# Carrying a product along in the feed-forward cycles instead of computing it again, for half of the tokens

## What is computed

```python
def _twist(x):                      # x in four parts of 64
    o_r, o_i, p_r, p_i = jnp.split(x, 4, axis=-1)
    return jnp.concatenate([p_r, -p_i, -o_r, o_i], axis=-1)

gf = _global_net(x.mean(axis=1, keepdims=True), ...)
out = x
for _ in range(3):                  # NUM_CYCLES
    h = _gelu(out @ w1 + b1)        # 256 -> 256, the "first product"
    h = _gelu(h @ w2 + b2)          # 256 -> 128
    h = _gelu(h @ w3 + b3)          # 128 -> 64
    tf = jax.nn.sigmoid(h @ w4 + b4)            # 64 -> 1
    coupling = 0.1 + adaptive_range * (0.7 * gf + 0.3 * tf - 0.5) * 2.0
    out = out + coupling * _twist(out)
```

## Time and profile before

| | |
|---|---|
| Median of 3 runs | 707.27 us (706.72 to 709.48) |
| The profiled execution | 706.14 us, of which the trace's span is 704.3 us |
| PE busy | 688.3 us (98%) |
| DVE busy | 384.4 us (55%) |
| ACT busy | 287.6 us (41%) |
| Granted PE clock, mean | 0.999 of full speed |

### The profile page before, as it was taken

How to read it: one execution, slowest core, us unless ns; L and a number is a source line. 1 busy time by engine, 2 the same in 40 slices (tenths; PEclk the granted TensorE clock), 3 DMA queues, 4 the chain that set the end, 5 groups by cost and what they waited for, 6 DMA issues and landing times.

```text
span 704.3 us, 11180 instructions
## 1 busy us (share of the span) xinstructions
PE 688.3 (98%) x3616; PEld 475.1 (67%) x3617; DVE 384.4 (55%) x951; ACT 287.6 (41%) x599; POOL 132.9 (19%) x111
## 2 busy tenths in 40 slices
PE   8999999999999999999999999999999999999996
PEld 7777777776754444688999746656556777777765
DVE  4688877788724454788777657212333333333331
ACT  3555434543544655766777541110323222222220
POOL 3100000000000000600000104661123334333333
PEclk9999999999999999999999999999999999999999
DMA  9781000000052000004800201423582666666643
GB/s 292 194 250 34 1 0 0 0 0 0 1 167 73 0 5 5 1 1 167 312 0 1 89 2 49 140 86 113 171 222 30 166 153 175 168 164 164 165 101 35
DMA packets 54934, 65.15 MB, mean 92 GB/s; under 512 B 11583, under 2 KB 37905, under 8 KB 54895
## 3 DMA queue, kind: packets, MB, share of 16 engines
q1 hardware_dynamic: 47806, 55.31, 24.6%
q0 software_dynamic: 7088, 9.35, 7.7%
HBM read 48.48 MB, written 16.00 MB: 92 GB/s over the span
## 4 chain that ended last, share of the span: by engine, by line
PE 92%; DVE 3%; ACT 1%; issue 1%; DMA 1%; POOLq 0%; SPq 0%; DVEq 0%; ACTq 0%; POOL 0%
PE ps L567 82%; PE ps L570 10%; DVE stats L1701 1%; DMA early<-in_wk 1%; DVE x_rows L1965 0%; POOLq L133 0%; ACT work L1285 0%; DVE work L1992 0%; DMA work<-expert_rows 0%; DVE x_rows L2001 0%; DVE work L1834 0%; DVE maxes L1832 0%; ACT early L1448 0%; ACT middle L1319 0%; DVE rden L1990 0%
## 5 line engine op out<-in xcount | busy, mean ns | idle before, releaser
L567 PE MATMUL ps<-middle,work 128*128 128x256 f32 (+4 forms) x656 | 177.4, 420 | 1.2 <-ACT work L1285 0.8
L1285 ACT ACTIVATE work<-ps 128x512 f32<-128x512 f32 (+3 forms) x209 | 83.1, 437 | 200.3 <-PE ps L570 183.6
L567 PEld LDWEIGHTS ps<-middle,work 128*128 128x128 f32 (+1 forms) x656 | 115.7, 183 | 48.3 <-issue 29.2
L567 PE MATMUL ps<-late,work 32*128 32x154 f32 (+5 forms) x880 | 141.9, 345 | 0.6 <-ACT work L1285 0.6
L533 POOL DMA_INDIRECT out_rows<-masks x47 | 70.4, 1498 | 152.3 <-DMA out_rows<-masks 56.7
L567 PEld LDWEIGHTS ps<-late,work 128*128 128x128 f32 (+2 forms) x880 | 92.1, 178 | 6.4 <-issue 3.4
L567 PE MATMUL ps<-work,late 128*128 128x256 f32 (+1 forms) x416 | 83.0, 352 | 0.6 <-ACT work L1285 0.5
L570 PE MATMUL ps<-consts_sb,work 128*128 128x128 f32 (+1 forms) x564 | 80.1, 275 | 1.8 <-DVE work L1992 1.2
L499 POOL TENSOR_TENSOR rstd<-var_eps,minus_half 128x8 f32<-128x8 f32 (+1 forms) x10 | 13.9, 1392 | 358.1 <-DVE var_eps L1716 358.1
L570 PEld LDWEIGHTS ps<-consts_sb,work 128*128 128x128 f32 (+1 forms) x564 | 65.1, 140 | 22.0 <-issue 11.6
L567 PE MATMUL ps<-early,late 128*128 128x512 f32 (+2 forms) x192 | 77.6, 608 | 0.3 <-ACT early L1435 0.3
(11 more groups left out here) (226 smaller groups left out, 720.4 us busy)
## 6 DMA issues: line engine op xcount, KB each, us to landing
late<-in_w SPq DMA_DIRECT2D x40, 512.0 KB
early<-in_w SPq DMA_DIRECT2D x16, 512.0 KB, 9.7
expert_rows<-work SPq DMA_DIRECT2D x36, 130.0 KB, 2.9
work<-expert_rows SPq DMA_DIRECT2D x36, 130.0 KB
middle<-in_w SPq DMA_DIRECT2D x8, 512.0 KB, 7.9
out_rows<-x_rows SPq DMA_DIRECT2D x4, 512.0 KB, 3.2
x_rows<-in_x SPq DMA_DIRECT2D x2, 768.0 KB, 10.6
late<-in_ws SPq DMA_DIRECT2D x3, 512.0 KB, 4.0
```

The source lines that it names most:

```text
L567: return nc.tensor.matmul(o, l, r, start=start, stop=stop, **kw)
L1285: return nc.scalar.activation(o, i, ACT.Copy)
```

## The change

For the second pair of groups the first product is computed from scratch only in the first cycle. There `net1` also computes a second product `z` from the same state with twisted weights `wz` (built once on DVE), which is `_twist(out) @ w1`. ACT copies both products out of PSUM (`keep_y`, `keep_z`). In the later cycles DVE forms the next first product from the kept ones: `turn_y(n)`: y + c z, and between the cycles `turn_z(n)`: z - c y. `act1` of steps 6, 7, 10 and 11 reads the result (`yn`) from SBUF. The state of the second pair is still updated, but nobody on PE waits for it before the end, so its updates move to the back of DVE's list. The first pair keeps computing its products with `net1`.

So PE loses `net1` of steps 6, 7, 10 and 11 (eight calls) and gains four calls for `z` of steps 2 and 3. ACT gains eight copies. DVE gains four small operations for `wz`, four `turn_y` and two `turn_z`, each of the latter four operations of 128x512. `su1` moves to other banks and other places. The orders on all three engines are written out anew, and the two `keep_warm` matmuls stand behind `net3(5)` and `net4(5)`.

```diff
+FIRST = [("y", 0), ("y", 1), ("y", 2), ("y", 3), ("z", 2), ("z", 3), ("y", 4), ("y", 5), ("y", 8), ("y", 9)]
+UPDATES = [0, 1, 4, 5, 2, 3, 6, 8, 9, 7, 10, 11]
...
+        ys = cut(early, 4096, [2, 2, G4]); zs = cut(early, 6144, [2, 2, G4])
+        yn = cut(work, 4608, [2, 2, G4]); turn_u = [cut(work, 3584 + 512 * o, [G4]) for o in range(2)]
+        wz = cut(masks, 1600, [KD, 256])
...
-            def net1(n, o):
+            def net1(n, o, kind="y"):
                 g = ffn_group(n)
-                pe.wait_ge(q["f_upd"], n + 1)
+                if kind == "z":
+                    pe.wait_ge(q["f_ev"], n - 1)
+                elif n < NG:
+                    pe.wait_ge(q["f_upd"], n + 1)
+                else:
+                    pe.wait_ge(q["f_upd"], updated(n - NG))
+                    pe.wait_ge(q["f_ev"], 3 + n % 2)
...
             def net2(n):
                 pe.wait_ge(q["f_a1"], 2 * n + 2)
+                after(pe, q["f_a2"], n - 1)
...
             net2(2)
+            net1(2, 0, "z")
+            net1(2, 1, "z")
             pe.wait_ge(q["f_gact"], 3)
             net2(3)
-
-            for p in range(2, 6):
-                net1(2 * p, 0)
-                net3(p - 1)
-                net1(2 * p, 1)
-                net4(p - 1)
-                net1(2 * p + 1, 0)
-                net1(2 * p + 1, 1)
-                net2(2 * p)
-                net2(2 * p + 1)
-                if p < 4:
-                    su1(p - 2)
-
-            to_rows(0, 0, 0)
-            net3(5)
-            to_rows(0, 1, 6)
-            to_rows(1, 0, 4)
-            to_rows(1, 1, 5)
-            net4(5)
+            net1(3, 0, "z")
+            net1(3, 1, "z")
+            net1(4, 0)
+            net3(1)
+            net1(4, 1)
+            net4(1)
+            net1(5, 0)
+            net1(5, 1)
+            net2(4)
+            net2(5)
+            su1(0)
+            net3(2)
+            su1(1)
+            net4(2)
+            net2(6)
+            net2(7)
+            net3(3)
+            net1(8, 0)
+            net4(3)
+            net1(8, 1)
+            net1(9, 0)
+            net1(9, 1)
+            net2(8)
+            net2(9)
+            net2(10)
+            net3(4)
+            net2(11)
+            net4(4)
...
-            keep_warm(2, 1)
+            net3(5)
+            keep_warm(1, 1)
+            net4(5)
+            keep_warm(1, 1)
+            to_rows(0, 0, 0)
+            to_rows(1, 0, 4)
+            to_rows(0, 1, 6)
+            to_rows(1, 1, 5)
...
             def act1(n, o):
-                act.wait_ge(q["f_l1"], 2 * n + o + 1)
-                nc.scalar.activation(h1[n % 2][:, o, :], ps[:, 4 * (n % 2) + o, :], ACT.Gelu,
+
+                after(act, q["f_l2"], n - 1)
+                if ("y", n) in FIRST:
+                    act.wait_ge(q["f_l1"], first_product("y", n, o))
+                    src = ps[:, 4 * (n % 2) + o, :]
+                else:
+                    act.wait_ge(q["f_y"], turned_y(n, o))
+                    src = yn[:, n % 2, o, :]
+                nc.scalar.activation(h1[n % 2][:, o, :], src, ACT.Gelu,
...
+            def keep_y(n, o):
+
+                last = copy(ys[:, n % 2, o, :], ps[:, 4 * (n % 2) + o, :])
+                if o == 1:
+                    last.then_inc(q["f_ev"], 1)
+
+            def keep_z(n):
+
+                for o in range(2):
+                    act.wait_ge(q["f_l1"], first_product("z", n, o))
+                    last = copy(zs[:, n % 2, o, :], ps[:, 4 * (n % 2) + o, :])
+                last.then_inc(q["f_ev"], 1)
...
             act2(2)
+            keep_z(2)
             act2(3)
-            for p in range(2, 6):
...
+            keep_z(3)
+            act1(4, 0)
...
+            act2(5)
+            act1(6, 1)
+            act3(2)
+            act1(7, 0)
+            act1(7, 1)
+            act4(4)
+            act4(5)
+            act2(6)
+            act2(7)
+            act3(3)
+            act1(8, 0)
+            act4(6)
+            act4(7)
+            act1(8, 1)
+            act1(9, 0)
+            act1(9, 1)
+            act1(10, 0)
+            act2(8)
+            act1(10, 1)
+            act2(9)
+            act1(11, 0)
+            act3(4)
+            act1(11, 1)
+            act2(10)
+            act2(11)
+            act4(8)
+            act4(9)
             act3(5)
             act4(10)
             act4(11)
...
+            def turn_y(n):
+
+                k, c = n % 2, tt[n - NG]
+                dve.wait_ge(q["f_a4"], n - NG + 1)
+                dve.wait_ge(q["f_ev"], 3 + k)
+                seq.mark(v.tensor_tensor(turn_u[0], c, zs[:, k, 0, :], ALU.mult))
+                seq(v.tensor_tensor(turn_u[1], c, zs[:, k, 1, :], ALU.mult))
+                for o in range(2):
+                    v.tensor_tensor(yn[:, k, o, :], (ys if n < 2 * NG else yn)[:, k, o, :], turn_u[o],
+                                    ALU.add).then_inc(q["f_y"], 1)
+                dve.wait_ge(q["f_y"], turned_y(n, 1))
+
+            def turn_z(n):
+
+                k, c = n % 2, tt[n]
+                seq.mark(v.tensor_tensor(turn_u[0], c, ys[:, k, 0, :], ALU.mult))
+                seq(v.tensor_tensor(turn_u[1], c, ys[:, k, 1, :], ALU.mult))
+                for o in range(2):
+                    seq.mark(v.tensor_tensor(zs[:, k, o, :], zs[:, k, o, :], turn_u[o], ALU.subtract))
+                seq.sync()
...
-            for n in range(10):
-                update(n)
...
+            update(0)
+            update(1)
+            turn_y(6)
+            turn_y(7)
+            seq(v.tensor_reduce(odd, con[:, C_BD:C_BD + 8].rearrange("p (a j) -> p j a", j=2), AX.X, ALU.add))
+            su1_build(0)
+            turn_z(2)
+            su1_build(1)
+            update(4)
+            update(5)
+            turn_z(3)
+            turn_y(10)
+            turn_y(11)
+            update(2)
+            update(3)
+            update(6)
+            update(8)
+            update(9)
+            update(7)
             ffn_out(0, 0, 0, 1)
             ffn_out(1, 0, 4, 2)
             variances(5)
```

More of the change, by code:

```diff
@@ L201, in build @@
         h3 = [cut(early, 11264 + 512 * p, [G4]) for p in range(2)]
-        tt = [cut(early, 12288 + 512 * p, [G4]) for p in range(2)]
+        tt = {n: cut(early, 12288 + 512 * (n % 2), [G4]) for n in (0, 1, 4, 5, 8, 9)}
+        tt |= {n: cut(work, 1536 + 256 * (n - n % 2 - 2) + 512 * (n % 2), [G4]) for n in (2, 3, 6, 7)}
+        tt |= {n: cut(early, 8192 + 1024 * (n % 2), [G4]) for n in (10, 11)}
+        ys = cut(early, 4096, [2, 2, G4]); zs = cut(early, 6144, [2, 2, G4])
+        yn = cut(work, 4608, [2, 2, G4]); turn_u = [cut(work, 3584 + 512 * o, [G4]) for o in range(2)]
+        wz = cut(masks, 1600, [KD, 256])
         cs = cut(early, 13312, [G4]); u0 = cut(early, 13824, [G4]); u1 = cut(early, 14336, [G4])
@@ L1445, in act4 @@
                 act.wait_ge(q["f_l4"], n + 1)
-                if n >= 2:
-                    act.wait_ge(q["f_upd"], n + 3)
-                last = nc.scalar.activation(tt[b], ps[:, 7 - 4 * b, :], ACT.Tanh, bias=hb[:, 1:2], scale=0.5)
+                if n >= NG and n % 4 < 2:
+                    act.wait_ge(q["f_upd"], updated(n - NG))
+                last = nc.scalar.activation(tt[n], ps[:, 7 - 4 * b, :], ACT.Tanh, bias=hb[:, 1:2], scale=0.5)
                 if n >= 2:
@@ L1452, in act4 @@
                     act.wait_ge(q["f_tanh"], n - 1)
-                    last = nc.scalar.activation(tt[b], tt[b], ACT.Identity, bias=cpl[:, 1 + b:2 + b], scale=cpl[:, 0:1])
+                    last = nc.scalar.activation(tt[n], tt[n], ACT.Identity, bias=cpl[:, 1 + b:2 + b], scale=cpl[:, 0:1])
                 last.then_inc(q["f_a4"], 1)
@@ L1471, in _ @@
             act1(2, 0)
+            keep_y(2, 0)
             act.wait_ge(q["f_gmm"], 1)
@@ L1474, in _ @@
             act1(2, 1)
+            keep_y(2, 1)
             act.wait_ge(q["f_gmm"], 2)
@@ L1483, in _ @@
             act1(3, 1)
+            keep_y(3, 1)
             act2(2)
+            keep_z(2)
             act2(3)
-            for p in range(2, 6):
-                act1(2 * p, 0)
-                act3(p - 1)
-                act1(2 * p, 1)
-                act4(2 * p - 2)
-                act4(2 * p - 1)
-                act1(2 * p + 1, 0)
-                act1(2 * p + 1, 1)
-                act2(2 * p)
-                act2(2 * p + 1)
+            keep_z(3)
+            act1(4, 0)
+            act3(1)
+            act1(4, 1)
+            act4(2)
+            act4(3)
+            act1(5, 0)
+            act1(5, 1)
+            act2(4)
+            act1(6, 0)
+            act2(5)
[25 more added lines that the diff above has]
+            act4(9)
             act3(5)
@@ L1811, in su1_build @@
                 else:
-                    last = v.tensor_copy(vtok.rearrange("p b d -> p (b d)"), ps[0:NK, 7, :])
+                    last = v.tensor_copy(vtok.rearrange("p b d -> p (b d)"), ps[0:NK, 4, :])
                 last.then_inc(q["su1_dve"], 1)
```

(6 more changed lines are left out.)

52 lines of the change are left out of this document (27 added, 25 removed).

## The result

| | before | after |
|---|---|---|
| median of the runs | 707.00 us (4 runs, 705.75 to 709.48) | 715.23 us (4 runs, 714.84 to 715.59) |
| profiled execution, its span | 706.14, 704.3 us | 715.59, 713.8 us |
| mean granted clock of PE | 0.999 | 0.984 |

The kernel is slower by about 1.1%: the ratio is 1.0107 (95% interval 1.0084 to 1.0129), and the two medians are 8.2 us apart (1.16%). The time is 4.0 us over the forecast of 711.2. It lies inside the whole range (707.0 to 716.0), but outside the forecast's own range (709.7 to 712.7) and inside that of the first rival, the clock that falls in the hole (712.5 to 716).

The account below looks back on a forecast made before the run. PE was taken to bound the feed-forward stage up to its tail, where it waits for others. Stalls 2.75 plus tail 1.17 gave +3.9 us: 710.0 for the profiled execution, 711.2 in the median, range 707.0 to 716.0.

Parts of the forecast that it names:

- first rival: PE's clock halves in the hole at the stage's end, into the second attention: 2 to 4 us, 712.5 to 716, chance 0.25.
- PE gains nothing up to T: From net2(2) to the result of net4(4), PE has 21 calls before and after the change.
- T: The tanh of step 8, last coupling of the first pair: 270.41 us before, predicted at 273.16 after.
- three stalls: PE waits for ACT's gelus ahead of net4(4): 0.85 at net3(3), 0.5 at net2(10), 1.4 at net2(11), sum 2.75 us.
- The 6.88 us: PE loses eight calls and gains four, 4 x 1.72 us, taken from the calls behind the tanh of step 8.
- Three updates: On DVE, updates 8, 9 and 7 at 2.66 us each put ffn_out(0,0) at T + 9.68.
- 5.50 us: From ffn_out(0,0) to PE's columns1: three ffn_out with statistics, one with variances(5), then xn0, reaching T + 15.18.
- A stall of some 3 us before `net3(5)` and a hole of some 6 us: In the tail PE waits for both act4, then for DVE about 6 us with one small seed matmul in it.
- After `columns1` all moves by the same amount: Order behind the first columns1 is unchanged, so the rest keeps its length and shifts by the sum, 3.9 us.
- Rival 2: The tail's chain has room, so columns1 comes up to 6.88 us earlier: 700.4 with the whole gain, chance 0.10.
- rival 3: The stalls ahead of net4(4) vanish, the tail's +1.2 us stays: 708.4; with in-between cases chance 0.15.
- Rival 4: Turned products come late or ACT's copies stall PE before 245 us: +1 to +3, 712 to 714, chance 0.05.

Follow-up runs that it names:

- early_dve: after with net2(10), net2(11) behind net4(4), two transposes ahead of net4(5), update(7) ahead of update(8), and matmuls without a reader in the holes: 708.4 us.
- late7: early_dve with update(7) on DVE moved behind variances(6), after the first normalized tiles: 706.52 us, ratio to before 0.9974.
- u7: after with update(7) moved ahead of update(8) on DVE: 713.79 us; the _warm version also fills PE's holes with matmuls without a reader: 708.91 us.
- warm_both: after with matmuls without a reader added in both of PE's holes: 710.09 us, ratio to before 1.0038.
- warm_first: after with three matmuls without a reader before net3(5) only, in the first hole: 714.05 us in one run.
- warm_second: after with matmuls without a reader in the second hole only, behind the last to_rows and the seed matmul: 711.41 us in one run.
- late7_su: late7 with net2(6) ahead of net4(2) and su1(1) behind net2(7), so net3(3) comes one su1 later: 706.96 us.
- early_pool: early_dve with updates 2, 3, 6 and 7 given from DVE to POOL, with scratch of its own: 712.78 us.

## Why the prediction was right, and where it was short

The measured time lies in the range because the range took in the first rival. The forecast itself, with the clock unchanged, missed by 4.0 us; its account of the order of work held, and what it left out is point 5.

1. *PE gains nothing up to T; three stalls.* Right. T predicted 273.16, measured 272.94. The stalls: 0.85 predicted, 0.78 measured; 0.5 and 0.28; 1.4 and 1.40. Sum 2.75 against 2.46. The gelu out of SBUF, which no row of before had, takes 0.71 us; 0.684 was taken.
2. *The 6.88 us are taken out of the cover of the tail.* Two calls put back behind `net4(4)` bring T 3.5 us forward and fill the hole before `net3(5)` (early_dve, late7). By itself that gains little over u7_warm (708.4 against 708.91); with the update out of the tail as well the time is 706.5.
3. *Three updates, then 5.50 us, to `columns1` at T + 15.18.* Right at full clock: T + 15.16, 15.16 and 15.15 in warm_both, warm_first and warm_second; u7_warm takes one update away and gets 1.6 of its 2.66 us. In after itself it was T + 16.16, 1.0 of it the clock's, through the late transposes.
4. *A stall of some 3 us before `net3(5)` and a hole of some 6 us.* Right: 3.25 us; in warm_first PE's idle around the seed matmul is 2.79 + 2.93 = 5.7 us. In after the late transposes take up part of the second hole, 1.15 + 2.93 = 4.1 are left.
5. *After `columns1` all moves by the same amount.* Wrong, and here the forecast failed. It took the clock as it was and gave the rest of the stage the time of before; the runs showed 23.59 us instead of 18.83. Together with the 1.0 of point 3 the clock costs 5.1 us by medians (after against warm_both), where the first rival said 2 to 4. Behind the start of the next stage the assumption held: the shift of after against before is 9.44 us at `ffn_out` of group 2 and 9.65 at DVE's last instruction. (One reading beside it was off: the transposes at 302.61 in the earlier trace rows read the update of step 10, done at 292.94, not POOL's last one. The slack was larger than 4.3 us, and nothing in the sum hangs on it.)

Why was the rival's price short? It was costed in one hole and over 5 us. There were two holes, since the 3.25 us that I had worked out as a stall made the clock fall as well, and behind the second it stayed low for 13 us, far into the next stage. The rival's chance of 0.25 was also low: the `keep_warm` just before and the small seed matmul in the hole, put down against it, did not hold the clock in the second hole of any kernel that left it unfilled (after, warm_first, u7). With the clock held, the forecast stands: the profiled execution of warm_both is 4.0 us over that of before, forecast 3.9; its median 2.8 over, as the medians of before lie 1.1 over its profiled execution, raised by the executions with a lower clock (708 to 711 us).

Rival 2 (the cover holds) and rival 3 (stalls vanish, 708.4) fell with T and `columns1`. Rival 4 fell too: no copy of ACT and no turned product holds PE up before 245 us; the first stall that the change makes is the one that ends at 252.37.

*Open:* why a hole of 3.25 us let the clock fall in after and u7 and not in warm_second, while one of 2.28 us did in early_dve. The traces of after, u7 and warm_second show the same waits in it. The prices of the two holes, 1.2 and 4.0 us, are of one run of warm_first against medians. Of the three stalls only the first was undone, in late7_su and not in after. What makes the last few us of an execution 1.5 us longer or shorter is not shown.

## What to carry to other kernels

When work is taken away from the bounding engine, find where in its order the missing calls stood and what they covered; what is gone there is cover, and up to that place nothing is gained. Look then at the idle it leaves on PE: here two holes of 3 and 4 us cost more through the clock (5.1 us) than the later order of the work did (2.8 to 4.0, warm_both over before), and a few matmuls without a reader took it all back. An update that has to be done somewhere can be worth putting behind the chain that ends the stage: here the next stage gave back 1.0 of 1.7 us. And before a gain of half a us is believed, the clocks of the executions on both sides have to be compared.

## What the runs showed of the hardware that I had not expected

- **DVE and POOL hinder each other in plain float32 additions and products.** A `tensor_tensor` of 128x512 with both inputs in SBUF takes DVE 0.68 us alone and 1.6 to 1.8 beside POOL's (early_pool). POOL takes 1.27 for it in before and 1.6 to 1.8 beside DVE's; only the first one at 237.49, which started 0.01 us ahead of DVE's, kept its 1.27. The Trainium skill, "SBUF — State Buffer", "Who interferes with whom", says that a DVE instruction with two SBUF inputs contends with a GpSimd instruction that reads SBUF. The trace agrees. A POOL that is busy 19% of the span is no free room while DVE has such work: side by side four operations on each took 6.7 us (271.36 to 278.02 on DVE), and DVE alone takes 5.3 for eight of them (two updates).
- **The low clock outlasts its cause.** In after some 5.5 us at 0.50 followed the end of a hole of 3 us, some 13 that of one of 4 us, with PE busy for the whole of the stretches at 278 and 300. In u7 the first fall lasted 3.4 us in all instead of 6.8, and in warm_second the same hole did not make the clock fall.
